# Int8 values transposed in pairs: a per-batch linear layer, layer norm and a quantised feed-forward on one core

## The chip, the cores and the metric

The kernel runs on one core of one Trainium2 chip. The metric is the time of one launch in microseconds (us) of device time. Three runs of the kernel before took 373.23, 369.0 and 368.7 us; the median is 369.0 us.

## What is computed

There are 8 batches of 256 tokens with 1024 features. Each batch picks one of 16 weight matrices by its id; the result is normalised, then goes through two linear layers whose inputs and weights are rounded to 255 levels with one scale per row, with a gelu between them. The input is added at the end.

```
w = weight[adapter_ids]                      # (8, 1024, 1024), float32
y = einsum('bij,bkj->bik', x, w)             # x: (8, 256, 1024)

def fake_quant(x):                           # one scale for each row
    s = maximum(max(abs(x), -1) / 127.0, 1e-8)
    return clip(round(x / s), -127, 127) * s

h = layernorm(y) * gamma + beta
h = einsum('bti,oi->bto', fake_quant(h), fake_quant(w1)) + b1
h = gelu(h, approximate=False)
h = einsum('bti,oi->bto', fake_quant(h), fake_quant(w3)) + b3
return x + h
```

## The kernel before, in words

**Sizes.** Tokens are cut into `TT` = 2 tiles of 128 rows, features into `CB` = 8 blocks of 128 columns, outputs into `KH` = 2 halves of 512, which is one PSUM bank of float32.

**First layer.** x and w are each split into a high part (the engine's float32r format) and the rest, and a product is three matmuls, hi\*hi, hi\*lo and lo\*hi (`products`, lines 1080 to 1082). A weight matrix is 4 units of 256 output rows; each unit has two pieces (`k` = 0, 1). For batches 2 to 7 a unit is loaded by SP (`load_unit`, line 285), transposed from `w_nat` into PSUM (`t_ps`) by VectorE in 32x32 blocks (`transpose_w`, line 803), copied to `w_hi` by ScalarE (`split_w`, line 574) and subtracted into `w_lo` by VectorE (`low_w`, line 809). x goes the same way (lines 296, 818, 580), except that GpSimd subtracts (`low_x`, line 483). For batches 0 and 1 TensorE transposes in float32 (`transpose_first`, lines 1173 and 1186).

**Norm.** ScalarE copies a half of y out of PSUM (`copy_y`, line 589), VectorE takes the statistics, GpSimd works out the scale and shift (`normalisers`), ScalarE applies them (`normalise`, line 593), and GpSimd multiplies by gamma and adds beta (`scale_and_shift`, lines 458 and 460).

**Quantisation.** VectorE takes the maximum of each row and its inverse (`scales_h`, `scales_g`, `max_prep` and `scales_prep`). The rounding is one instruction that multiplies by the inverse and adds MAGIC = 12582912.0, after which the low 16 bits of each float32 are the rounded value as an int16. It is ScalarE's for h and g (`round_h` line 601, `round_h_last` line 607, `round_g` line 622, and lines 707 and 711 in the last period) and GpSimd's for the 16 tiles of 128 rows of w1 and w3 (`round_prep`, line 489). TensorE transposes those low halves as bf16 bit patterns, 8 blocks of 128x128 for each tile of 128 rows (`transpose_tile`, line 1111), into one PSUM bank of 1024 16-bit words. ScalarE copies the bank as int16 to bf16 (`take_h` line 613 for two tiles at once, `take_g` line 627, `take_prep` line 639, `take` line 685 in the last period) into `q_t` or `w_q`. The products of the two linear layers are bf16 matmuls (`product_half`, line 1134): `ffn1` of h with w1, `ffn2` of g with w3.

**After the products.** `rescale1` (VectorE, line 876) scales the first product, `add_b1` (GpSimd, line 478) adds the bias, `gelu` (ScalarE, line 618) follows; `scale_ffn2` (ScalarE, line 632) scales the second, and `finish` (GpSimd, lines 466 and 469) multiplies by the row of weight scales and adds x + b3, which `residual` made (line 474). `store` (SP, line 359) writes it out.

**Order.** Each engine has its own list, written out by hand, and engines wait for each other by semaphores only. Batches 0 and 1 and the preparation of w1 and w3 stand in a start part written out step by step. Then comes a loop `period(p)` for p = 2 to 6, in which the first layer of batch p and p+1 and the feed-forward of batch p-1 are interleaved, and then a last period in which batches 6 and 7 are finished. In a period GpSimd runs `low_x(p+1, 0)`, `add_b1(p-1, 0)`, `residual`, `normalisers`, `low_x(p+1, 1)`, `add_b1(p-1, 1)`, two `scale_and_shift`, two `finish`. On SP the load of unit 1 of batch p+2 stands behind the store of the first tile of batch p-1. On TensorE a period is 8 pieces of the first layer, four transposed tiles (two of h, two of g) and the four products of the feed-forward:

```
            def period(p):                      # TensorE
                piece(p, 2, 0)
                transpose_h(p - 1, 0)
                transpose_h(p - 1, 1)
                piece(p, 2, 1)
                ffn1(p - 1, 0)
                ...
                piece(p + 1, 0, 0)
                transpose_g(p - 1, 0)
                piece(p + 1, 0, 1)
                ffn2(p - 1, 0)
```

Of the kernel before, what the change touches and what calls it, by code (L numbers as in the profile page):

```python
# [5 lines left out]
F32 = mybir.dt.float32  # L6
F32R = mybir.dt.float32r
BF16 = mybir.dt.bfloat16
I16 = mybir.dt.int16
# [5 lines left out]
P = 128  # L15
# [6 lines left out]

MAGIC = 12582912.0


def adaln_ffn_kernel(nc, x, ids, weight, gamma, beta, w1, b1, w3, b3, out):
# [27 lines left out]
    RT = D // P  # L54
    PREP = 2 * RT
# [6 lines left out]
    CONSTS = 7  # L62
# [3 lines left out]
    with ExitStack() as ctx:  # L66
# [30 lines left out]
        magic = sb("magic", [P, 1], F32)  # L97
# [34 lines left out]

        a_ps = psum("a_ps", [P, TT, BANK])
# [141 lines left out]
        def _(sp):  # L275
# [109 lines left out]
            load_prep((2, 4))  # L385
# [5 lines left out]
            load_prep((3, 5))  # L391
            load_rows_of_w((1,))
            load_prep((6,))
            load_rows_of_w((2, 5))
# [3 lines left out]
            load_prep((7, 8, 9))  # L398
            load_rows_of_w((4, 6, 7))
            load_prep((12, 10))  # L400
# [3 lines left out]
            load_prep((15, 14))  # L404
# [32 lines left out]
        def _(pool):  # L437
# [48 lines left out]
            def round_prep(tiles):  # L486
                for i in tiles:
                    pool.wait_ge(wq_inv_ready, part_of(i) + 1)
                    pool.tensor_scalar(prep_slot[i], prep_slot[i], wq_inv[:, i:i + 1], magic[:],
                                       ALU.mult, ALU.add).then_inc(wq_rounded, 1)  # L490

            def period(p):
# [6 lines left out]
                for t in range(TT):  # L499
                    scale_and_shift(p, t)  # L500
                for t in range(TT):
                    finish(p - 1, t)
# [3 lines left out]
            pool.memset(magic[:], MAGIC).then_inc(consts_ready, 1)  # L506
# [12 lines left out]
            round_prep((0, 1, 2, 3, 4, 5, 6))  # L519
# [5 lines left out]
            round_prep((9, 10, 11, 12))  # L525
# [5 lines left out]
            round_prep((14, 15))  # L531
# [28 lines left out]
        def _(act):  # L560
# [35 lines left out]
            def round_h(f, t):  # L596
                act.wait_ge(h_inv_ready, TT * f + t + 1)
                if isinstance(f, int) and f == 0:
                    act.wait_ge(first_transposed, first_piece(10, 0) + 1)
                wait_past(act, h_transposed, TT * (f - 1) + t + 1)  # L600
                act.activation(h_r[:, t, :], rows_of(f)[:, t, :], ACT.Identity, scale=h_inv[:, t:t + 1], bias=magic[:]
                               ).then_inc(h_rounded, 1)

            def round_h_last(t):
                act.wait_ge(h_inv_ready, TT * LAST + t + 1)
                act.wait_ge(h_transposed, TT * (LAST - 1) + t + 1)
                act.activation(h_r[:, t, :], y[:, t, :], ACT.Identity, scale=h_inv[:, TT + t:TT + t + 1], bias=magic[:]
                               ).then_inc(h_rounded, 1)
# [38 lines left out]
            def period(p):  # L647
                both(p + 1, 0)
                take_h(p - 1)
                split_x(p + 1, 0)  # L650
                both(p + 1, 1)
# [24 lines left out]
            def last_period():  # L676
# [6 lines left out]
                def take(ready, n, bank, blocks, done):  # L683
                    act.wait_ge(ready, n)
                    act.activation(blocks, transposed(bank, I16), ACT.Copy).then_inc(done, 1)
# [15 lines left out]
                for half in range(KH):  # L701
# [5 lines left out]
                act.activation(a_last[:, 0], a_last[:, 0], ACT.Identity, scale=g_inv[:, TT:TT + 1], bias=magic[:]  # L707
                               ).then_inc(g_rounded, 1)
                take(g_transposed, TT * LAST + 1, t_ps[:, 1, 0], q_last[:, 1, 0], g_t_ready)
                act.wait_ge(g_inv_ready, TT * LAST + 2)  # L710
                act.activation(a_last[:, 1], a_last[:, 1], ACT.Identity, scale=g_inv[:, TT + 1:TT + 2], bias=magic[:]
                               ).then_inc(g_rounded, 1)
# [659 lines left out]
```

## Time and profile before

| | |
|---|---|
| runs, us | 373.23, 369.0, 368.7 (median 369.0) |
| span of the profiled execution, us | 372.5 |
| TensorE (PE) busy | 341.4 us, 92% of the span, 1854 records |
| weight loads (PEld) busy | 235.9 us, 63% |
| VectorE (DVE) busy | 285.5 us, 77% |
| GpSimd (POOL) busy | 263.4 us, 71% |
| ScalarE (ACT) busy | 227.1 us, 61% |
| chain of waits | POOL 41%, issue 22%, DMA 13%, DVE 11%, PE 7%, SP's queue 3%, ACT 2% |

The profiled execution has no time of its own beside its span; the span is 0.7 us below the first of the three runs and 3.5 us above the median. "Issue" in the chain of waits is time in which an engine waited for nothing that the profile shows.

In the views below times are counted from the start of the span. A line of the timeline gives start and length in us, engine, line of the kernel, operation, what is written and read, the count of merged instructions and, in brackets, how long the engine sat idle before it and what ended the wait. The length of merged matmuls includes the end of the last one, which overlaps the next instruction; the pace is the distance from start to start. A few matmul records are missing, so that 16 matmuls can show as 15.

### The profile page before, as it was taken

The page shows a single profiled execution, that of the slowest core. Times are in us where ns is not written, and L with a number is a line of the kernel's source. Part 1 is how long each engine was busy: PE and PEld are TensorE (multiplying, and loading weights), DVE is VectorE, ACT ScalarE, POOL GpSimd, SP SyncE. Part 2 cuts the span into 40 slices and gives each one's busy share as a digit, 9 for nine tenths or more (in the row PEclk, how much of TensorE's full clock was granted, in tenths as well). Part 3 has the DMA queues.
Part 4 walks back from the last instruction along what each step waited for, and adds up shares of the span by engine and source line. Part 5 has one row for each costly group of instructions (what it writes and reads, how often), then busy time and mean ns, then how long its engine had stood idle before and what let it go on. Part 6 is the DMA issues. An engine that isn't in the chain of part 4 may idle for free.

```text
span 372.5 us, 5769 instructions
## 1 busy us (share of the span) xinstructions
PE 341.4 (92%) x1854; PEld 235.9 (63%) x1880; DVE 285.5 (77%) x344; ACT 227.1 (61%) x232; POOL 263.4 (71%) x164
## 2 busy tenths in 40 slices
PE   6898899996976999999999999999899989999885
PEld 6787788754763666666665666566566666674442
DVE  1459698886946777798778886888779687999866
ACT  2433476854888647773777658755777477625651
POOL 1402259841998579995999599968997699946831
PEclk9999999999899999999999999999999999999989
DMA  6999998695950899539971999099925990150014
GB/s 186 352 347 352 410 280 164 147 246 117 241 99 0 199 276 218 100 119 294 221 154 63 299 223 203 0 268 244 220 56 158 288 229 0 58 171 1 0 55 172
DMA packets 46203, 67.35 MB, mean 181 GB/s; under 512 B 2918, under 2 KB 37734, under 8 KB 46186
## 3 DMA queue, kind: packets, MB, share of 16 engines
q1 hardware_dynamic: 46186, 67.14, 68.8%
q8 instruction: 9, 0.15, 0.2%
q14 instruction: 8, 0.07, 0.1%
HBM read 58.74 MB, written 8.39 MB: 180 GB/s over the span
## 4 chain that ended last, share of the span: by engine, by line
POOL 41%; issue 22%; DMA 13%; DVE 11%; PE 7%; SPq 3%; ACT 2%; POOLq 0%; DVEq 0%
POOL y L458 8%; POOL x_res L474 7%; POOL o L466 6%; POOL y L460 5%; DMA x_res<-in_L_ffn_w 5%; POOL a L478 4%; POOL x_lo L483 4%; POOL o L469 3%; DMA w_scale_row<-in_L_ffn_w 3%; PE t_ps L1134 2%; DMA h_r<-in_L_cond_weight 2%; DVE x_nat L917 2%; DMA x_t<-in_L_ffn_b 2%; DVE wq_max L861 2%; DMA w_nat<-in_L_cond_weight 2%
## 5 line engine op out<-in xcount | busy, mean ns | idle before, releaser
L1080 PE MATMUL a_ps<-w_hi,x_hi 128*128 128x512 f32 x256 | 107.5, 420 | 2.4 <-DVE w_lo L794 1.2
L1082 PE MATMUL a_ps<-w_hi,x_lo 128*128 128x512 f32 x256 | 100.8, 394 | 0.0
L1081 PE MATMUL a_ps<-w_lo,x_hi 128*128 128x512 f32 x256 | 100.7, 393 | 0.0
L1134 PE MATMUL f_ps<-w_q,q_t 128*128 128x512 bf16 x377 | 88.1, 379 | 9.7 <-ACT q_t L627 8.2
L1134 PEld LDWEIGHTS f_ps<-w_q,q_t 128*128 128x128 bf16 x400 | 37.1, 98 | 57.5 <-ACT q_t L627 12.5
L803 DVE STREAM_TRANSPOSE t_ps<-w_nat 128x1024 f32<-128x1024 f32 x48 | 57.5, 1238 | 11.7 <-DMA w_nat<-in_L_cond_weight 11.5
L809 DVE TENSOR_TENSOR w_lo<-t_ps,w_hi 128x1024 fp32r<-128x1024 f32 x48 | 57.2, 1219 | 8.9 <-ACT w_hi L574 8.7
L574 ACT ACTIVATE w_hi<-t_ps 128x1024 fp32r<-128x1024 f32 x48 | 49.0, 1023 | 21.9 <-DVE t_ps L803 21.1
L1080 PEld LDWEIGHTS a_ps<-w_hi,x_hi 128*128 128x128 f32 x256 | 48.5, 189 | 15.7 <-ACT y L589 3.2
L1082 PEld LDWEIGHTS a_ps<-w_hi,x_lo 128*128 128x128 f32 x256 | 48.5, 189 | 10.7
L1081 PEld LDWEIGHTS a_ps<-w_lo,x_hi 128*128 128x128 f32 x256 | 48.6, 190 | 9.0
L478 POOL TENSOR_TENSOR a<-a,rows 128x1024 f32<-128x1024 f32 x14 | 33.4, 2385 | 19.7 <-DVE a L876 17.5
L483 POOL TENSOR_TENSOR x_lo<-x_t,x_hi 128x1024 fp32r<-128x1024 f32 x12 | 28.7, 2395 | 20.8 <-ACT x_hi L580 20.8
L474 POOL TENSOR_TENSOR x_res<-x_res,rows 128x1024 f32<-128x1024 f32 x14 | 33.4, 2412 | 0.0
L466 POOL TENSOR_TENSOR o<-o,w_scale_row 128x1024 f32<-128x1024 f32 x12 | 28.5, 2379 | 3.7 <-ACT o L632 3.7
L469 POOL TENSOR_TENSOR o<-o,x_res 128x1024 f32<-128x1024 f32 x12 | 29.6, 2465 | 0.9
L460 POOL TENSOR_TENSOR y<-y,rows 128x1024 f32<-128x1024 f32 x12 | 28.7, 2391 | 0.9
L458 POOL TENSOR_TENSOR y<-y,rows 128x1024 f32<-128x1024 f32 x12 | 28.6, 2382 | 0.0
L852 DVE TENSOR_REDUCE g_max<-a 128x1 f32<-128x1024 f32 x14 | 17.0, 1218 | 14.8 <-ACT a L618 14.8
L844 DVE TENSOR_REDUCE h_max<-y 128x1 f32<-128x1024 f32 x14 | 17.1, 1218 | 14.6 <-POOL y L460 14.6
L618 ACT ACTIVATE a<-a 128x1024 f32<-128x1024 f32 x14 | 14.8, 1056 | 16.4 <-POOL a L478 16.4
L569 ACT ACTIVATE w_hi<-t_ps 128x1024 fp32r<-128x1024 f32 x14 | 14.2, 1027 | 17.1 <-PE t_ps L1173 11.0
(151 smaller groups left out, 503.1 us busy)
## 6 DMA issues: line engine op xcount, KB each, us to landing
w_nat<-in_L_cond_weight SPq DMA_DIRECT2D x96, 256.0 KB, 6.5
x_res<-in_x SPq DMA_DIRECT2D x7, 1024.0 KB, 6.3
out<-o SPq DMA_DIRECT2D x14, 512.0 KB, 3.1
x_nat<-in_x SPq DMA_DIRECT2D x24, 256.0 KB, 9.9
w_nat<-in_L_cond_weight SPq DMA_DIRECT2D x10, 512.0 KB, 8.9
w_q<-in_L_ffn_w SPq DMA_DIRECT2D x4, 512.0 KB, 7.9
h_r<-in_L_cond_weight SPq DMA_DIRECT2D x4, 512.0 KB, 6.7
w_scale_row<-in_L_ffn_w SPq DMA_DIRECT2D x3, 512.0 KB, 10.3
```

The source lines that it names most:

```text
L458: pool.tensor_tensor(row, row, gamma_row, ALU.mult).then_inc(gamma_done, 1)
L460: pool.tensor_tensor(row, row, beta_row, ALU.add).then_inc(h_ready, 1)
L466: pool.tensor_tensor(o[:, t, :], o[:, t, :], w_scale_row[:, 1, :], ALU.mult).then_inc(out_scaled, 1)
L474: pool.tensor_tensor(x_res[:, t, :], x_res[:, t, :], b3_row, ALU.add).then_inc(x_b3_ready, 1)
L478: pool.tensor_tensor(a[:, t, :], a[:, t, :], b1_row, ALU.add).then_inc(ffn1_biased, 1)
L574: act.activation(part_of_unit(w_hi, u, k), piece_bank(k), ACT.Copy).then_inc(w_hi_ready, 1)
L803: dve.transpose(piece_bank(k).rearrange("p c (kb s) -> p kb c s", s=BLK), w_nat[:, u % 2].rearrange("p kb (c r) -> p kb c r", r=BLK)[:, :, ...
L809: dve.tensor_tensor(part_of_unit(w_lo, u, k), piece_bank(k), part_of_unit(w_hi, u, k).bitcast(F32), ALU.subtract).then_inc(w_lo_ready, 1)
L1080: pe.matmul(ps, hi, w_hi[:, u, c], start=begin, stop=False)
L1081: pe.matmul(ps, hi, w_lo[:, u, c], start=False, stop=False)
L1082: last = pe.matmul(ps, lo, w_hi[:, u, c], start=False, stop=end)
L1134: last = pe.matmul(ps[:, half, :], q[:, c, :], w[:, c, half_of(half)], start=c == 0, stop=c == CB - 1)
```

## The change

Rounded values are written as int8 by the rounding instruction itself: it multiplies by the inverse scale and the write converts, with no constant added. Two neighbouring bytes make one 16-bit word, so that a tile of 128 rows is 512 words, and TensorE transposes 4 blocks of 128x128 words in place of 8. ScalarE copies the transposed words out byte by byte: block 2c + b takes byte b of each word of block c, so it reads every second byte of PSUM and writes bf16. Activations and weights get the same order of rows in the product. `take_h` finds both tiles in one bank. h and g lie in byte ranges of `h_r`, so that `a` is no longer overwritten by the rounding. The constant `magic` and its memset go. Calls on several tiles are written out one by one; the order of the steps on each engine stays.

```diff
-I16 = mybir.dt.int16
+I8 = mybir.dt.int8
...
+    PACK = 2
-    CONSTS = 7
+    CONSTS = 6
...
+        bytes_of = [h_r[:, t, :].bitcast(I8) for t in range(TT)]
+        h_8 = [row[:, 0:D] for row in bytes_of]
+        g_8 = [row[:, D:2 * D] for row in bytes_of]
+        g_8_last = [row[:, 2 * D:3 * D] for row in bytes_of]
+        prep_8 = [slot.bitcast(I8)[:, 0:D] for slot in prep_slot]
...
-        def transposed(bank, dtype):
-            return bank.bitcast(dtype).rearrange("p (c k) -> p c k", k=P)
+        WORDS = D // PACK // PACK
+        def words_of(bank, t=0):
+            return bank[:, WORDS * t:WORDS * (t + 1)].bitcast(BF16).rearrange("p (c k) -> p c k", k=P)
+        def bytes_in(bank, tiles=1):
+            return bank[:, 0:WORDS * tiles].bitcast(I8).rearrange("p (c k b) -> p c b k", k=P, b=PACK)
+        def blocks_in(q):
+            return q.rearrange("p (c b) k -> p c b k", b=PACK)
...
-                    pool.tensor_scalar(prep_slot[i], prep_slot[i], wq_inv[:, i:i + 1], magic[:],
-                                       ALU.mult, ALU.add).then_inc(wq_rounded, 1)
+                    pool.tensor_scalar(prep_8[i], prep_slot[i], wq_inv[:, i:i + 1], None, ALU.mult).then_inc(wq_rounded, 1)
...
-            pool.memset(magic[:], MAGIC).then_inc(consts_ready, 1)
...
-                act.activation(h_r[:, t, :], rows_of(f)[:, t, :], ACT.Identity, scale=h_inv[:, t:t + 1], bias=magic[:]
-                               ).then_inc(h_rounded, 1)
+                act.activation(h_8[t], rows_of(f)[:, t, :], ACT.Identity, scale=h_inv[:, t:t + 1]).then_inc(h_rounded, 1)
...
-                act.activation(q_t[:].rearrange("p t c k -> p (t c k)"),
-                               f_ps[:].bitcast(I16).rearrange("p h n -> p (h n)"), ACT.Copy).then_inc(h_t_ready, 1)
+                act.activation(blocks_in(q_t[:].rearrange("p t c k -> p (t c) k")), bytes_in(f_ps[:, 0], TT), ACT.Copy
+                               ).then_inc(h_t_ready, 1)
...
-                act.activation(a[:, t, :], a[:, t, :], ACT.Identity, scale=g_inv[:, t:t + 1], bias=magic[:]
-                               ).then_inc(g_rounded, 1)
+                act.activation(g_8[t], a[:, t, :], ACT.Identity, scale=g_inv[:, t:t + 1]).then_inc(g_rounded, 1)
...
-                act.activation(q_t[:, t], transposed(f_ps[:, 0], I16), ACT.Copy).then_inc(g_t_ready, 1)
+                act.activation(blocks_in(q_t[:, t]), bytes_in(f_ps[:, 0]), ACT.Copy).then_inc(g_t_ready, 1)
...
-                    act.activation(w_q[i // RT][:, :, rows_of_tile], transposed(f_ps[:, i % 2], I16), ACT.Copy
+                    act.activation(blocks_in(w_q[i // RT][:, :, rows_of_tile]), bytes_in(f_ps[:, i % 2]), ACT.Copy
...
-            def transpose_tile(src, bank, done):
-                halves = src.bitcast(BF16).rearrange("p (k two) -> p k two", two=2)[:, :, 0]
-                blocks = transposed(bank, BF16)
-                for c in range(CB):
-                    last = pe.transpose(blocks[:, c, :], halves[:, c * P:(c + 1) * P], ident_16[:])
+            def transpose_tile(src, blocks, done):
+                words = src.bitcast(BF16)
+                for c in range(CB // PACK):
+                    last = pe.transpose(blocks[:, c, :], words[:, c * P:(c + 1) * P], ident_16[:])
                 last.then_inc(done, 1)
...
-                transpose_tile(h_r[:, t, :], f_ps[:, t], h_transposed)
+                transpose_tile(h_8[t], words_of(f_ps[:, 0], t), h_transposed)
...
-                transpose_tile(a[:, t, :], f_ps[:, 0], g_transposed)
+                transpose_tile(g_8[t], words_of(f_ps[:, 0]), g_transposed)
```

The last period's rounding, transposing and copying change in the same way, with `g_8_last` for the last batch's g.

## Rows read from the trace of the kernel before

**Rows 1.** The page, busy time, share of the span and instructions of each engine.
```profile
PE 341.4 (92%) x1854; PEld 235.9 (63%) x1880; DVE 285.5 (77%) x344; ACT 227.1 (61%) x232; POOL 263.4 (71%) x164
```

**Rows 2.** Stretches: from:to, length, PE busy (records), granted clock, DMA share, GB/s.
```profile
92.90:96.30 3.40, 3.40 (x10) 0.50 0.67 184
211.14:250.80 39.66, 38.20 (x191) 1.00 0.78 183
355.70:359.10 3.40, 3.40 (x15) 0.50 0.00 0
```

**Rows 3.** Timeline of one loop period, GpSimd, SP's queue and VectorE.
```profile
214.32 2.42 POOL L478 TENSOR_TENSOR a<-a,rows 128x1024 f32<-128x1024 f32 x1 [1.29 <-DVE a L876]
239.40 2.39 POOL L469 TENSOR_TENSOR o<-o,x_res 128x1024 f32<-128x1024 f32 x1
...
242.96 1.85 SPq L285 DMA_DIRECT2D w_nat<-in_L_cond_weight  x4
250.78 2.39 DVE L803 STREAM_TRANSPOSE t_ps<-w_nat 128x1024 f32<-128x1024 f32 x2 [1.75 <-DMA w_nat<-in_L_cond_weight]
254.53 2.40 POOL L478 TENSOR_TENSOR a<-a,rows 128x1024 f32<-128x1024 f32 x1 [1.85 <-DVE a L876]
```

**Rows 4.** Waits of SP's queue: us in total, times, longest.
```profile
SPq L359 <- POOL o L469: 123.1, 12, 26.1
```

**Rows 5.** Timeline of the same period, TensorE and ScalarE.
```profile
233.21 0.62 PE L1111 MATMUL f_ps<-ident,a 128*128 128x128 bf16 x8
233.63 0.48 PE L1080 MATMUL a_ps<-w_hi,x_hi 128*128 128x512 f32 x1
...
240.94 0.50 PE L1080 MATMUL a_ps<-w_hi,x_hi 128*128 128x512 f32 x1 [0.30 <-ACT y L589]
245.45 1.87 ACT L613 ACTIVATE q_t<-f_ps 128x2048 bf16<-128x2048 int16 x1
247.75 3.40 PE L1134 MATMUL f_ps<-w_q,q_t 128*128 128x512 bf16 x15
```

**Rows 6.** Groups by line: busy us, mean ns of one, idle before and its releaser.
```profile
L601 ACT ACTIVATE h_r<-y,magic,h_inv 128x1024 f32<-128x1024 f32 x12 | 14.9, 1244 | 11.3 <-DVE h_inv L840 11.3
L632 ACT ACTIVATE o<-f_ps,g_scale 128x1024 f32<-128x1024 f32 x12 | 13.3, 1109 | 2.3 <-PE f_ps L1134 2.3
L639 ACT ACTIVATE w_q<-f_ps 128x1024 bf16<-128x1024 int16 x16 | 16.0, 1023 | 6.2 <-PE f_ps L1111 6.2
L489 POOL TENSOR_SCALAR w_q<-w_q,wq_inv,magic 128x1024 f32<-128x1024 f32 x4 | 4.8, 1202 | 16.1 <-DVE wq_inv L840 16.1
L460 POOL TENSOR_TENSOR y<-y,rows 128x1024 f32<-128x1024 f32 x12 | 28.7, 2391 | 0.9
L505 POOL MEMSET ident<- 128x128 bf16 x1 | 0.2, 205 | 0.0
L504 POOL MEMSET ident<- 128x128 f32 x1 | 0.2, 205 | 0.3 <-POOLq L1362 0.3
```

**Rows 7.** Timeline of the start part, four engines.
```profile
70.89 1.25 ACT L601 ACTIVATE h_r<-y_first,magic,h_inv 128x1024 f32<-128x1024 f32 x1
88.08 1.22 DVE L861 TENSOR_REDUCE wq_max<-w_scale_row 128x1 f32<-128x1024 f32 x1 [1.56 <-DMA w_scale_row<-in_L_ffn_w]
104.16 1.07 PE L1111 MATMUL f_ps<-ident,y_first 128*128 128x128 bf16 x16
116.92 2.35 POOL L466 TENSOR_TENSOR o<-o,w_scale_row 128x1024 f32<-128x1024 f32 x1 [0.92 <-ACT o L632]
```

**Rows 8.** ScalarE in the start part, the same columns as rows 2 with ACT busy.
```profile
97.09:116.84 19.75, 17.40 (x17) 1.00 0.52 112
```

**Rows 9.** Timeline of the last period.
```profile
355.37 3.29 PE L1134 MATMUL t_ps<-w_q,q_t 128*128 128x512 bf16 x8 [2.74 <-ACT q_t L685]
358.46 0.94 PE L1111 MATMUL t_ps<-ident,w_nat 128*128 128x128 bf16 x8
359.23 1.89 PE L1134 MATMUL t_ps<-w_q,q_t 128*128 128x512 bf16 x8
```

More of the change, by code:

```diff
@@ L397, in _ @@
             load_rows_of_w((3,))
-            load_prep((7, 8, 9))
-            load_rows_of_w((4, 6, 7))
-            load_prep((12, 10))
+            load_prep((7,))
+            load_prep((8,))
+            load_prep((9,))
+            load_rows_of_w((4,))
+            load_rows_of_w((6,))
+            load_rows_of_w((7,))
+            load_prep((12,))
+            load_prep((10,))
             load_unit(2, 1)
@@ L498, in period @@
                 add_b1(p - 1, 1)
[L499 to L502, printed above, removed]
+                scale_and_shift(p, 0)
+                scale_and_shift(p, 1)
+                finish(p - 1, 0)
+                finish(p - 1, 1)
             pool.memset(ident[:], 0.0).then_inc(consts_zeroed, 1)
             pool.memset(ident_16[:], 0.0).then_inc(consts_zeroed, 1)
-            pool.memset(magic[:], MAGIC).then_inc(consts_ready, 1)
             pool.memset(minus_half[:], -0.5).then_inc(consts_ready, 1)
@@ L518, in _ @@
                 pool.partition_broadcast(rows[:, k], rows_1[k]).then_inc(rows_ready, 1)
-            round_prep((0, 1, 2, 3, 4, 5, 6))
+            round_prep((0,))
+            round_prep((1,))
+            round_prep((2,))
+            round_prep((3,))
+            round_prep((4,))
+            round_prep((5,))
+            round_prep((6,))
             normalisers_of(0)
@@ L647, in period @@
             def period(p):
-                both(p + 1, 0)
+                split_w(p + 1, 0, 0)
+                split_w(p + 1, 0, 1)
                 take_h(p - 1)
                 split_x(p + 1, 0)
-                both(p + 1, 1)
+                split_w(p + 1, 1, 0)
+                split_w(p + 1, 1, 1)
                 gelu(p - 1, 0)
@@ L684, in take @@
                     act.wait_ge(ready, n)
-                    act.activation(blocks, transposed(bank, I16), ACT.Copy).then_inc(done, 1)
+                    act.activation(blocks_in(blocks), bytes_in(bank), ACT.Copy).then_inc(done, 1)
                 take_h(f)
@@ L756, in _ @@
             split_x(2, 0)
-            both(2, 1)
+            split_w(2, 1, 0)
+            split_w(2, 1, 1)
             gelu(0, 0)
@@ L884, in period @@
             def period(p):
-                both(transpose_w, p + 1, 0)
-                both(low_w, p + 1, 0)
+                transpose_w(p + 1, 0, 0)
+                transpose_w(p + 1, 0, 1)
+                low_w(p + 1, 0, 0)
+                low_w(p + 1, 0, 1)
                 transpose_x(p + 1)
-                both(transpose_w, p + 1, 1)
+                transpose_w(p + 1, 1, 0)
+                transpose_w(p + 1, 1, 1)
                 rescale1(p - 1, 0)
-                both(low_w, p + 1, 1)
+                low_w(p + 1, 1, 0)
+                low_w(p + 1, 1, 1)
                 scales_g(p - 1, 0, a[:, 0, :], 0)
@@ L894, in period @@
                 rescale1(p - 1, 1)
-                both(transpose_w, p + 1, 2)
+                transpose_w(p + 1, 2, 0)
+                transpose_w(p + 1, 2, 1)
                 low_w(p + 1, 2, 0)
@@ L899, in period @@
                 scales_h(p, 0, 0)
-                both(transpose_w, p + 1, 3)
+                transpose_w(p + 1, 3, 0)
+                transpose_w(p + 1, 3, 1)
                 scales_h(p, 1, 1)
-                both(low_w, p + 1, 3)
+                low_w(p + 1, 3, 0)
+                low_w(p + 1, 3, 1)
                 statistics(p + 1, 0)
@@ L1037, in _ @@
             scales_h(0, 1, 1)
-            both(transpose_w, 2, 0)
+            transpose_w(2, 0, 0)
+            transpose_w(2, 0, 1)
             low_w(2, 0, 0)
@@ L1061, in _ @@
             scales_h(1, 0, 0)
-            both(low_w, 2, 3)
+            low_w(2, 3, 0)
+            low_w(2, 3, 1)
             scales_h(1, 1, 1)
@@ L1250, in last_period @@
                 pe.wait_ge(y_copied, UNITS * LAST + TT + 1)
-                transpose_tile(h_r[:, 0, :], a_ps[:, 0], h_transposed)
+                transpose_tile(h_8[0], words_of(a_ps[:, 0]), h_transposed)
                 product_half(q_t[:, 1], w_q[0], t_ps[:, 0], 1, ffn1_done)
@@ L1315, in _ @@
             piece(1, 0, 0)
-            prepare((4, 5))
+            prepare((4,))
+            prepare((5,))
             piece(1, 0, 1)
```

69 lines of the change are left out of this document (40 added, 29 removed).

## Prediction

> **What bounds the kernel now.** I read the page's busy shares first: TensorE at 92% of the span against VectorE's 77% looks like the bound [rows 1], and the loop seems to agree, since a period of 39.66 us holds 38.20 us of TensorE work at full clock [rows 2]. If that were all, each transpose taken away would come off the time. So the second view is the timeline of one loop period, read for what each engine waits on. GpSimd starts `add_b1(0)` at 214.32 and then runs without a gap that matters to the end of the first `finish` at 239.40 + 2.39 = 241.79, some 27.5 us. SP issues the load of unit 1 of the next batch at 242.96, VectorE sits idle until that load has landed and starts its transposes at 250.78, and GpSimd's next `add_b1(0)`, which waits for VectorE's rescaled product, starts at 254.53 [rows 3]. That is a closed ring of 254.53 - 214.32 = 40.2 us: 27.5 GpSimd, 9.0 store, issue and DMA, 3.75 VectorE. The other four periods of the loop begin the same way. SP's waits confirm the joint: its queue stood 123.1 us behind the `finish` [rows 4], with the load of unit 1 queued right behind the store. TensorE is not in this ring. It runs nearly as long as the ring does, and falls into step once a period, where its next first-layer piece waits for a ScalarE copy that itself waits on GpSimd's rows (at 240.94) [rows 5]. So in the loop TensorE is nearly full, but it follows.
>
> The start part is loads first (VectorE waits on a landing at 88.08), then from about 92 to 117 TensorE, ScalarE and GpSimd side by side, at whose end GpSimd waits 0.92 us for ScalarE's `scale_ffn2` [rows 7]. The last period is one chain through all engines, ending in TensorE's last products.
>
> **The change, part by part.**
>
> *Transposes.* Eight of them take 233.63 - 233.21 = 0.42 us from their start to the next piece [rows 5], about 53 ns each; four cost half, so a tile saves 0.21 us. There are 16 weight tiles, 16 of h and 16 of g: 48 tiles, 10.1 us of TensorE time in all. The new source is contiguous where the old one took every second 16-bit word; both give 128 columns of 16 bits, and I keep the price per transpose. Where it counts:
> - Loop, five periods, four tiles each: 0.84 us a period. Nothing in the ring waits for it; TensorE waits longer for the copies instead. 0.
> - Start before 88: the tile transposes lie between waits for loads. What can pass on is that `round_h(0, 1)` at 70.89, which releases the loads of the last w3 tiles, comes after copies that wait for TensorE, with some three tiles ahead of it. Its own gain below included, 0 to 0.8 us; as the landing at 88.08 also depends on loads that do not move, I take 0.3.
> - Start, 92 to 117: seven weight tiles (9 to 15) are transposed, among them two in the 16 of 104.16, so TensorE gets 1.5 us ahead. GpSimd can gain at most its 0.92 us wait [rows 7], for it is busy back to back before that. Bounds 0 and 0.92; I take 0.8, since ScalarE's own list then comes last. As the first store leaves earlier by this, the loop begins earlier by it.
> - Last period: one tile at 358.46 stands between two products, at half clock, 359.23 - 358.46 = 0.77 us [rows 9]; half goes, 0.38. One more stands before the last batch's second tile's product, at full clock: 0.21. The others there end before a wait. 0.59 in all; bounds 0 and 0.8.
>
> *ScalarE's rounding.* It took 1244 ns with a scale and a bias tile; the same function with the scale alone takes 1109 ns [rows 6], so 0.135 us less. The output is int8, which no row shows. Bounds: 0.2 less to 0.9 more (the latter if bytes were written at half speed, by the 0.86 us that 1024 elements more add, 1.87 against 1.023 [rows 5, 6]). I take 0.135 less, nearest to the same function's row. On the path lie two, both in the last period (h of the last tile, g of batch 6): 0.27. In the loop h and g's rounding lies beside the ring.
>
> *ScalarE's copies out of PSUM.* The element count stays; the read goes from contiguous int16 (1023 ns for 1024) [rows 6] to every second byte. Bounds: same, or half rate at +0.86 us a copy. I take the same, because stepping two bytes touches no more memory than the int16 did. The other end is a rival.
>
> *GpSimd's rounding of weights.* 1202 ns with two operations and two scalar operands; its two-input operation of the same size takes 2391 ns [rows 6], so the time follows what is read, and a bf16 memset takes the 205 ns of a float32 one [rows 6]. Bounds: 1.1 and 2.4 us. I take 1.2, no change. Most of the 16 end well before what waits on them; those for tiles 13 to 15, between 94 and 101, are in GpSimd's back-to-back stretch.
>
> *The rest.* One memset of a single column less, g rounded into `h_r` rather than in place, calls written out singly and one more register load on SP: all behind waits for loads, or without a new wait. The new buffer adds no semaphore. 0; if the extra SP step counted, tenths of a us.
>
> *Clock.* The granted clock fell to one half for 3.4 us at 92.9 and at 355.7 [rows 2], each time after TensorE had sat idle, the second after a wait of 2.74 us [rows 9] behind ScalarE and VectorE. The change lengthens such waits slightly, it does not remove them. A fall costs half of 3.4, 1.7 us of TensorE time. I leave both in place; one that vanished, or one more, is a bound of 1.7 either way.
>
> Sum: 0.3 + 0.8 + 0.59 + 0.27 = 2.0 us. It is worked out against an execution with a span of 372.5, 3.5 above the median; the ring's 40.2 against a period's 39.66 [rows 2, 3] is the kind of difference that it is made of. I take the difference off the median: 369.0 - 2.0 = **367.0 us**.
>
> **The rivals.**
>
> *TensorE sets the pace after all.* For it: 38.20 of 39.66 us busy [rows 2]. Then all 48 tiles count: 369.0 - 10.1 = 358.9, faster by 2.7%. Against it: the load, the two VectorE steps and `finish` have no TensorE in them, and GpSimd, whose wait it would have to shorten, waits for VectorE, which waits for a DMA.
>
> *Byte reads out of PSUM at half rate, slower than before.* Place: ScalarE's copies. In the loop `take_h` would end at 247.32 + 1.7 = 249.0 against the product's start at 247.75 [rows 5], about 1.3 us late. The first product can stand that (it is done by 251.15 and VectorE comes to it at 250.78 + 2.39 = 253.17 [rows 3, 5]); for the second I have 0 to 1.3 and take 0.4 us a period, 2.0 in all. In the start part six weight copies and the first of g, 7 x 0.86 = 6.0 us, meet 19.75 - 17.40 = 2.35 us of idle [rows 8]; 3.6 reach GpSimd. In the last period the copy that ended the 2.74 us wait [rows 9] adds 0.86 and two later ones about 0.5. 7.0 us: 367.0 + 7.0 = 374.0. It decides from about 0.25 us a copy, where it eats the 2.0 gained. For it: no row reads with a step. Against it: the int16 copy runs at the pace of float32 copies in the trace. The Trainium skill speaks for this rival, Advanced Engine Details and Errata, section PSUM Cachelines: the lines are 8 bytes, and "every two consecutive elements should be contiguous for best throughput". By that rule the new copies are the slow kind; the step is inside one line, though, and no row here shows a stepped read, so the trace neither confirms nor denies it.
>
> *GpSimd converts to int8 slowly.* Each rounding at the 2.4 us of its dearer operation, 1.2 more. The three on the path give 3.6 us; of the first nine, three stand before the first norm and can hold the loads behind `round_h(0, 1)` by up to 3 more. 370.6 to 373.6, say 372. Against it: the memset rows, and that one operation of two is gone.
>
> **How the numbers follow.** The forecast, a small gain through start and end alone, has 0.74; TensorE's pace 0.10; byte reads 0.08; GpSimd's conversion 0.08. The forecast's own bounds, all gains at their ends and the clock's 1.7 one way, reach from 364 to 371. I stretch to 363.5 and 372.0, which takes in half of GpSimd's rival and leaves out TensorE's pace and the byte reads: some 0.2 in all. 2% is 7.4 us, about what a measurement of this kernel can tell from no change. Faster by that is TensorE's pace, 0.10. Slower by that needs either slow rival at over its stated price, 0.04. Within 2%: 0.86.
>
> **What would show it.** Right: loop periods still 39.6 to 40.2 us with the same GpSimd and DMA joints, TensorE's records 192 fewer, its busy time some 10 us less and its idle time larger by about as much, the copies at 1.0 us, ScalarE's rounding near 1.1, GpSimd's at 1.2, and the loop entered about 1 us earlier. Wrong: loop periods shorter by 0.8 (TensorE's pace), copies of 1.9 us, or GpSimd rounding at over 1.5 us. A third fall of the clock, as TensorE idles more, would also show the sum short.

## The result, and the profile after

The change made the kernel slower: a median of 381.54 us (four runs, 380.74 to 383.4) against 371.12 us for the kernel before in runs alternated with it, a ratio of 1.031 with a 95% interval of 1.027 to 1.035 (one disturbed run of the kernel before, 472.58 us, is in its median but not in the ratio; below too, medians are of all runs and ratios of undisturbed ones). The prediction had 367.0 us and a range up to 372.0, so it missed by 14.5 us, 9.5 of them outside the range, and the sign was wrong: "slower by over 2%" had a chance of 0.04. The profiled execution took 380.74 us with a span of 378.9.

The page after, busy time and instructions of each engine, then the granted clock in 40 slices:

```profile
PE 333.1 (88%) x1667; PEld 225.7 (60%) x1688; DVE 284.4 (75%) x344; ACT 224.4 (59%) x232; POOL 289.2 (76%) x163
...
PEclk9999999699998999999999999999999999999989
```

Against [rows 1], TensorE has 187 records and 8.3 us less, as the change intends, and ScalarE 2.7 us less. GpSimd, with one instruction fewer, is busy 25.8 us longer. That one number says where to look. The groups by line say which instruction it is (busy us, mean ns of one, then the idle time before them):

```profile
L513 POOL TENSOR_SCALAR w_q<-w_q,wq_inv 128x1024 int8<-128x1024 f32 x4 | 11.3, 2850 | 15.5 <-DVE wq_inv L873 15.5
...
L668 ACT ACTIVATE w_q<-f_ps 128x1024 bf16<-128x1024 int8 x16 | 16.0, 1020 | 6.0 <-PE f_ps L1152 6.0
L633 ACT ACTIVATE h_r<-y,h_inv 128x1024 int8<-128x1024 f32 x12 | 13.8, 1150 | 14.7 <-DVE h_inv L873 14.7
L643 ACT ACTIVATE q_t<-f_ps 128x2048 bf16<-128x2048 int8 x7 | 13.1, 1873 | 2.4 <-PE f_ps L1152 2.4
```

A weight tile's rounding on GpSimd went from 1202 ns [rows 6] to 2850 (the other buffers' groups, 2836 to 2852 ns, are alike): 1.65 us more, sixteen times, 26.4 us. Everything else the change touched is as priced or close: ScalarE's byte reads take 1020 and 1873 ns, as the int16 reads did [rows 5, 6]; its rounding takes 1150 ns.

The extra time lies before the loop alone: the loop's first `add_b1(0)` starts at 141.87 us, against 135.05 before, 6.8 us later, and the spans are 6.4 apart (the profiled execution of the kernel before was one of its slower ones). A stretch of the kernel after, one period (from:to, length, TensorE busy and records, granted clock, DMA share, GB/s):

```profile
178.20:217.70 39.50, 37.16 (x175) 1.00 0.79 183
```

The period is what it was, with a microsecond less of TensorE work in it [rows 2]; from one `add_b1(0)` to the next the loop takes 39.5 to 40.3 us, where it took 39.6 to 40.2. And its joints are the same. The timeline of one period, GpSimd, SP's queue and VectorE:

```profile
221.50 2.40 POOL L502 TENSOR_TENSOR a<-a,rows 128x1024 f32<-128x1024 f32 x1 [1.76 <-DVE a L909]
246.60 2.38 POOL L493 TENSOR_TENSOR o<-o,x_res 128x1024 f32<-128x1024 f32 x1
...
250.15 1.86 SPq L300 DMA_DIRECT2D w_nat<-in_L_cond_weight  x4
...
257.58 2.39 DVE L836 STREAM_TRANSPOSE t_ps<-w_nat 128x1024 f32<-128x1024 f32 x2 [1.35 <-DMA w_nat<-in_L_cond_weight]
261.32 2.40 POOL L502 TENSOR_TENSOR a<-a,rows 128x1024 f32<-128x1024 f32 x1 [1.44 <-DVE a L909]
```

From `add_b1(0)` to the end of `finish` 27.5 us, then 8.6 of store, issue and DMA, then 3.74 of VectorE: 39.8 us, against 27.5, 9.0 and 3.75 in [rows 3].

### The profile page after: what moved, and what is told of

Read it like the earlier page. It is cut to its first block, busy times and chain, and to the rows that moved or that the text cites. A ratio compares the mean times of both kernels' runs of the same rounds, so it can differ in the third digit from the quotient of the medians.

```text
span 378.9 us, 5398 instructions
## 1 busy us (share of the span) xinstructions
PE 333.1 (88%) x1667; PEld 225.7 (60%) x1688; DVE 284.4 (75%) x344; ACT 224.4 (59%) x232; POOL 289.2 (76%) x163
## 4 chain that ended last, share of the span: by engine, by line
POOL 49%; issue 20%; DMA 9%; DVE 9%; PE 6%; SPq 3%; ACT 2%; POOLq 0%; DVEq 0%; ACTq 0%
POOL y L482 7%; POOL x_res L498 7%; POOL o L490 6%; POOL y L484 5%; POOL a L502 5%; POOL x_lo L507 4%; POOL o L493 3%; DMA a<-in_L_ffn_w 3%; DMA w_scale_row<-in_L_ffn_w 3%; POOL w_scale_row L513 2%; PE t_ps L1175 2%; DMA h_r<-in_L_cond_weight 2%; DVE x_nat L957 2%; DMA x_t<-in_L_ffn_b 2%; POOL y L513 1%
## 5 line engine op out<-in xcount | busy, mean ns | idle before, releaser
L836 DVE STREAM_TRANSPOSE t_ps<-w_nat 128x1024 f32<-128x1024 f32 x48 | 57.5, 1238 | 10.1 <-DMA w_nat<-in_L_cond_weight 9.9
L606 ACT ACTIVATE w_hi<-t_ps 128x1024 fp32r<-128x1024 f32 x48 | 48.9, 1022 | 20.1 <-DVE t_ps L836 19.0
L648 ACT ACTIVATE a<-a 128x1024 f32<-128x1024 f32 x14 | 14.8, 1054 | 17.8 <-POOL a L502 17.8
L513 POOL TENSOR_SCALAR w_q<-w_q,wq_inv 128x1024 int8<-128x1024 f32 x4 | 11.3, 2850 | 15.5 <-DVE wq_inv L873 15.5
```

Source lines behind the costliest of these rows:

```text
L606: act.activation(part_of_unit(w_hi, u, k), piece_bank(k), ACT.Copy).then_inc(w_hi_ready, 1)
L836: dve.transpose(piece_bank(k).rearrange("p c (kb s) -> p kb c s", s=BLK), w_nat[:, u % 2].rearrange("p kb (c r) -> p kb c r", r=BLK)[:, :, ...
```

## The experiments

Three theories stood after this. A: GpSimd is slow because it writes int8. B: a term other than GpSimd is in it (h and g's bytes, or TensorE's idling). C: GpSimd is slow because its second operation is gone. (The expectation for m_forms, written before C had its name, calls it Theory B, together with a second suspicion, that input and output overlap.) In those for e1, e2 and e3 Theory A stands for GpSimd's rounding as the whole loss, whatever its reason. Ratios are to the kernel before, run beside each (369.98, 370.31, 369.85 and 370.3 us in the four sets).

**m_forms: single instructions.** A list of forms, run through three times, each instruction after the one before has ended; VectorE and ScalarE start only when GpSimd is done.

```diff
+then(pool.tensor_scalar(o_f32[:], src[:], scale[:], bias[:], ALU.mult, ALU.add))
+then(pool.tensor_scalar(o_f32[:], src[:], scale[:], None, ALU.mult))
+then(pool.tensor_scalar(o_bf16[:], src[:], scale[:], None, ALU.mult))
...
+then(pool.tensor_scalar(o_i8[:], src[:], scale[:], None, ALU.mult))
+then(pool.tensor_copy(o2_i8[:], src[:]))
...
+act.activation(a_f32[:], src[:], ACT.Identity, scale=scale[:])
+act.activation(a_i8[:], src[:], ACT.Identity, scale=scale[:])
```

> This kernel computes nothing of the reference: it loads one tile of 128x1024 float32, runs single instructions on it by form, and stores the tile unchanged. The changed kernel's trace has GpSimd's scaling with int8 output at 2.85 us where the float32 form took 1.20. Theory A, the type written sets the price: here the float32 forms take 1.2 us with one or with two scalar operands, the int8 form 2.85, also into a tile of its own, and the rewrite in place is no dearer. Theory B, it is the dropped second operation or the overlap of input and output: then the float32 form with one operation is slow as well, or the int8 form is fast where the output is a tile of its own. Open under A: whether bf16, int16 and int32 outputs cost as float32 or as int8; whether VectorE's and ScalarE's int8 outputs cost more than their float32 ones (ScalarE near 1.15 us, as in the changed kernel).

The groups by line of that kernel:

```profile
L75 POOL TENSOR_SCALAR o_i<-src,scale 128x1024 int8<-128x1024 f32 x3 | 8.5, 2845 | 0.3
L71 POOL TENSOR_SCALAR o_f<-src,scale 128x1024 f32<-128x1024 f32 x3 | 8.5, 2845 | 0.3
L72 POOL TENSOR_SCALAR o_bf<-src,scale 128x1024 bf16<-128x1024 f32 x3 | 8.5, 2844 | 0.3
...
L70 POOL TENSOR_SCALAR o_f<-src,scale,bias 128x1024 f32<-128x1024 f32 x3 | 3.6, 1193 | 4.9 <-DMA inplace<-in_L_ffn_w 4.7
L102 ACT ACTIVATE a_i<-src,scale 128x1024 int8<-128x1024 f32 x3 | 3.5, 1151 | 0.1
L100 ACT ACTIVATE a_f<-src,scale 128x1024 f32<-128x1024 f32 x3 | 3.5, 1150 | 0.1
...
L76 POOL CAST o_i<-src 128x1024 int8<-128x1024 f32 x3 | 3.1, 1037 | 0.2
```

Theory A falls: the multiply alone takes 2845 ns with float32, bf16 and int8 output alike, and the plain cast to int8 takes 1037 (int16 and int32 output take 2843 and 2844). So does the suspicion of overlap: the multiply to int8 in place takes 2845 as well. What is fast is the form with a multiply and an add. On ScalarE int8 output costs the same as float32.

**m_forms2: what makes the form fast.** The same with other operands.

```diff
...
+then(pool.tensor_scalar(o_i8[:], src[:], scale[:], zero[:], ALU.mult, ALU.add))
+then(pool.tensor_scalar(o_i8[:], src[:], scale[:], 0.0, ALU.mult, ALU.add))
+then(pool.tensor_scalar(o_i8[:], src[:], 1500.0, 0.0, ALU.mult, ALU.add))
+then(pool.tensor_scalar(o_i8[:], src[:], 1500.0, None, ALU.mult))
...
+then(pool.tensor_scalar(o_f32[:], src[:], scale[:], None, ALU.add))
```

> Single instructions again, nothing of the reference. The first such kernel showed GpSimd's scaling at 2.84 to 2.85 us for every output type where the second operation is left out, and 1.19 with it. Theory C, the missing second operation sets the price: the int8 output with a multiply and an add of a zero column takes 1.2 us, in place too. Rival, int8 with two operations is slow as well. Open: whether a constant in place of the zero column, or of the scale, keeps the 1.2 us, and whether an add alone is as slow as a multiply alone.

```profile
L78 POOL TENSOR_SCALAR o_f<-src,scale 128x1024 f32<-128x1024 f32 x3 | 8.5, 2842 | 0.3
L76 POOL TENSOR_SCALAR o_i<-src 128x1024 int8<-128x1024 f32 x3 | 8.3, 2772 | 0.3
...
L73 POOL TENSOR_SCALAR o_i<-src,scale,zero 128x1024 int8<-128x1024 f32 x3 | 3.6, 1190 | 0.3
...
L74 POOL TENSOR_SCALAR o_i<-src,scale 128x1024 int8<-128x1024 f32 x3 | 3.3, 1113 | 0.3
...
L75 POOL TENSOR_SCALAR o_i<-src 128x1024 int8<-128x1024 f32 x3 | 3.1, 1044 | 0.3
```

Over both kernels, every tensor-scalar form with two operations takes 1.04 to 1.20 us (1195 ns in place), every form with one 2.77 to 2.85, whatever type is written, whether the operand is a column or a constant, and whether the operation is a multiply or an add. Why one operation takes longer than two no run shows.

**e7_two_ops: the changed kernel with a neutral second operation.**

```diff
-pool.tensor_scalar(prep_8[i], prep_slot[i], wq_inv[:, i:i + 1], None, ALU.mult)
+pool.tensor_scalar(prep_8[i], prep_slot[i], wq_inv[:, i:i + 1], zero[:], ALU.mult, ALU.add)
...
+pool.memset(zero[:], 0.0).then_inc(consts_ready, 1)
```

> The changed kernel, with one thing more: GpSimd's rounding to int8 multiplies and then adds a column of zeros, so that it has two operations again. Theory C: each rounding falls from 2.85 to 1.2 us and the whole loss of 3.1% goes: ratio 0.993 to 1.003, the weights' shorter transposes being worth under 1 us. Rival, the byte layout itself costs (int8 output, stepped reads, idle TensorE): it stays above 1.02.

367.36 us, ratio 0.992 [0.989, 0.995]. An add of zero, with all the rest of the change left in, takes the whole loss away and leaves a gain, 3.0 us by medians, somewhat more than expected. It was run once more:

> The changed kernel with two operations in GpSimd's rounding once more, beside its sister with longer weight transposes on the same chip. Its first ratio was 0.9919 and that of the kernel with every transpose doubled 1.0018, 2.6 us apart by their medians, where the prediction's terms give 0.8 (start) + 0.6 (last period) = 1.4 and 0.3 more through the loads. Expected again 0.989 to 0.995, with loop periods of 39.6 to 40.5 us.

366.72 us, 0.991 [0.987, 0.994]. The group of roundings in this kernel:

```profile
L514 POOL TENSOR_SCALAR w_q<-w_q,wq_inv,zero 128x1024 int8<-128x1024 f32 x4 | 4.7, 1199 | 16.0 <-DVE wq_inv L876 16.0
```

**e10_one_op: the kernel before with one operation.** The reverse: nothing of the change but the missing operation. It leaves out the added constant, so that the low halves which are transposed are not the rounded weights.

```diff
-pool.tensor_scalar(prep_slot[i], prep_slot[i], wq_inv[:, i:i + 1], magic[:],
-                   ALU.mult, ALU.add).then_inc(wq_rounded, 1)
+pool.tensor_scalar(prep_slot[i], prep_slot[i], wq_inv[:, i:i + 1], None, ALU.mult).then_inc(wq_rounded, 1)
```

> The kernel before, whose weight rounding on GpSimd leaves out the add of the constant (the low halves that are transposed then are not the rounded weights, so this part of the computation is wrong). No byte anywhere. Theory C: the dropped operation alone makes 11 to 13 us, ratio 1.028 to 1.036. Rival: under 1.01, and the bytes are to blame.

384.5 us, 1.038 [1.032, 1.045], 14.2 us more than before, where 11 to 13 were expected; the group of roundings, float32 written as before:

```profile
L489 POOL TENSOR_SCALAR w_q<-w_q,wq_inv 128x1024 f32<-128x1024 f32 x4 | 11.4, 2854 | 16.6 <-DVE wq_inv L839 16.6
```

One operation of one instruction carries the loss, with no byte in the kernel.

**e1_hg_bytes and e2_w_bytes: each half of the change alone.** e1 keeps bytes for h and g and gives the weights their old rounding and eight transposes; e2 does the opposite.

```diff
 e1, against the changed kernel:
-pool.tensor_scalar(prep_8[i], prep_slot[i], wq_inv[:, i:i + 1], None, ALU.mult)
+pool.tensor_scalar(prep_slot[i], prep_slot[i], wq_inv[:, i:i + 1], magic[:], ALU.mult, ALU.add)
...
-transpose_tile(prep_8[i], words_of(f_ps[:, i % 2]), wq_transposed)
+transpose_halves(prep_slot[i], f_ps[:, i % 2], wq_transposed)
 e2, against the changed kernel:
-transpose_tile(h_8[t], words_of(f_ps[:, 0], t), h_transposed)
+transpose_tile(h_r[:, t, :], f_ps[:, t], h_transposed)
...
-transpose_tile(g_8[t], words_of(f_ps[:, 0]), g_transposed)
+transpose_tile(a[:, t, :], f_ps[:, 0], g_transposed)
```

> h and g as bytes, as in the changed kernel; the weights rounded by GpSimd in float32 with the constant added and transposed as eight blocks of 16-bit halves, as before, in the byte pairs' order of rows. Theory A (GpSimd's int8 rounding is the whole loss): the weights' share of the change is gone, so the time is that of the kernel before or a little under: 0 to 1 us less, ratio 0.997 to 1.00. Theory B (the loss lies in the loop or the last period, in the clock or in the copies out of PSUM): it stays slow, 375 us or more. The loop's periods stay at 39.6 to 40.2 us under both, if the ring of GpSimd, store, load and VectorE sets them.

> Only the weights as bytes, rounded by GpSimd straight to int8 and transposed as four blocks; h and g as before (their halves read in the byte pairs' order). Theory A: the whole loss is here, 9 to 12 us over the kernel before, ratio 1.025 to 1.032, and the loop is entered 6 to 8 us late. Theory B: no more than 3 us over it.

e1: 371.95 us, 1.004 [0.999, 1.009], no difference that it could show, though 0 to 1 us less was expected. e2: 382.26 us, 1.031 [1.025, 1.037], the whole loss. B falls for h and g: the 32 tiles whose transposes were halved there bring nothing measurable, as the loop ring says. What their bytes could cost is at most the upper end of e1's interval, 3.3 us; e9 below, all bytes with the TensorE work of before, narrows that to 0.5% (1.8 us).

**e3_pad: the time without the bytes.** The kernel before, with two extra operations ahead of each rounding, sized so that the three take about as long as one slow one.

```diff
+for width in (D, 384):
+    part = prep_slot[i][:, 0:width]
+    pool.tensor_scalar(part, part, 1.0, 0.0, ALU.mult, ALU.add).then_inc(padded, 1)
+    pads.append(1)
+    pool.wait_ge(padded, len(pads))
```

> The kernel before with nothing changed but that GpSimd, ahead of each of the 16 roundings, multiplies the tile by one and adds zero over 1024 and over 384 columns: 1.20 + 0.45 us more for each, the length that the int8 output added. Theory A, the loss is GpSimd's time alone: 9 to 12 us slower, as the changed kernel, plus the 1 us or so that the changed kernel got back by shorter transposes and roundings. Rival, the int8 form also disturbs others (VectorE, the DMAs) beyond its own length: this kernel stays under 6 us slower.

384.29 us, 1.035 [1.028, 1.041], again somewhat more than the 10 to 13 us expected. The pads took 2 x 0.782 = 1.56 us a rounding:

```profile
L494 POOL TENSOR_SCALAR w_q<-w_q 128x1024 f32<-128x1024 f32 (+1 forms) x8 | 6.3, 782 | 17.4 <-DVE wq_inv L848 17.1
```

So 25 us more of GpSimd work at these places cost 14.3 us at the end, and e10's 26.4 cost 14.2. The loss needs nothing but GpSimd's time; the rival of a disturbance beyond it falls.

**e5_swap: is the store in the ring?** In the kernel before, SP's load of the next batch's unit 1 goes ahead of the store that waits for `finish`.

```diff
-store(p - 1, 0)
 load_unit(p + 2, 1)
+store(p - 1, 0)
...
-store(0, 0)
 load_unit(3, 1)
+store(0, 0)
```

> The kernel before, with the load of unit 1 of the next batch but one ahead of the store of the first tile on SP's queue, in the loop and at its start. If the loop's period is the ring of GpSimd, store, load and VectorE, VectorE's wait for that load of 1.1 to 1.8 us a period goes, and the five periods shorten by 1 to 1.5 us each, 5 to 7 us in all, until TensorE's 38.2 us is the bound: ratio 0.980 to 0.987. If TensorE sets the period already, nothing moves.

362.87 us, 0.977 [0.969, 0.984], 7.4 us less, a little beyond the 5 to 7 expected. Its timeline, three engines:

```profile
207.21 2.40 POOL L478 TENSOR_TENSOR a<-a,rows 128x1024 f32<-128x1024 f32 x1
...
209.07 21.98 SPq L285 DMA_DIRECT2D w_nat<-in_L_cond_weight  x12
234.75 5.61 SPq L359 DMA_DIRECT2D out<-o  x2
...
241.91 2.34 DVE L803 STREAM_TRANSPOSE t_ps<-w_nat 128x1024 f32<-128x1024 f32 x2
245.61 2.40 POOL L478 TENSOR_TENSOR a<-a,rows 128x1024 f32<-128x1024 f32 x1
```

The loads now stand before the stores, VectorE starts its transposes at 241.91 without a wait, and the period is 245.61 - 207.21 = 38.4 us. The ring of the prediction was real: opened at that joint, the four intervals from one `add_b1(0)` of the loop to the next take 38.4 us each in place of 39.6 to 40.2, together 5.9 us less.

**e8_two_ops_swap: both together.** e7 with e5's order.

> The changed kernel with two operations in GpSimd's rounding and, on SP's queue, the load of unit 1 ahead of the first store. The swap alone gave 0.9765 and loop periods of 38.4 us, the second operation 0.9919. If the two gains lie in different places (loop; start and last period) they add: ratio 0.965 to 0.973, 358 to 360 us, the periods staying at 38.4 us, which GpSimd and VectorE now set. If the shorter transposes are worth something in the loop once its ring is shorter, the periods fall under 38.2 us and the ratio under 0.965.

358.98 us, 0.972 [0.965, 0.978], 2.8% faster than the kernel before and the fastest that was run. One period (columns as for the stretches above):

```profile
203.00:241.40 38.40, 37.11 (x174) 1.00 0.80 184
```

It is 38.4 us again, as in e5, with 1 us less of TensorE work than before the change, so the shorter transposes are worth nothing in the loop even then. What sets the period now was not tried.

**e9_two_ops_t_twice and e12_w_t_twice: what the transposes are worth.** e9 is e7 with every group of four transposes issued twice, e12 with those of the weight tiles alone.

```diff
 e9, against e7:
-for c in range(CB // PACK):
+for c in [*range(CB // PACK)] * 2:
 e12, against e7:
-for c in range(CB // PACK):
+for c in [*range(CB // PACK)] * times:
...
-transpose_tile(prep_8[i], words_of(f_ps[:, i % 2]), wq_transposed)
+transpose_tile(prep_8[i], words_of(f_ps[:, i % 2]), wq_transposed, 2)
```

> The changed kernel with two operations in GpSimd's rounding, and each group of four transposes issued twice, into the same place: TensorE has the work of the kernel before again, with all else as bytes. If the shorter transposes are worth 1.7 us, in the start part and the last period alone, this takes 1 to 2 us more than with them single, ratio 0.994 to 0.999 to the kernel before, and the loop's periods stay at 39.6 to 40.2 us. If TensorE's time passes on fully it takes 10 us more, ratio 1.02.

> As its sister, but each group of four transposes of a weight tile (the 16 in the start part) is issued twice; those of h and g stay single. If the shorter transposes gain in the start part, most of the difference is here: 1 to 2.5 us over its sister. If they gain in the loop or the last period, under 0.5 us.

e9: 369.79 us, 1.002 [0.999, 1.005]; e12: 370.85 us, 1.003 [0.999, 1.007]. Doubling the weight tiles' alone takes back all that e11 (0.991 [0.987, 0.994], run beside e12) had gained, 370.85 - 366.72 = 4.1 us by medians, where 1 to 2.5 were expected. e9 against e7 is 2.4 us by medians, but those two ran in different sets; by their ratios it is 0.010, 3.7 us. Doubling those of h and g as well adds nothing that shows. The gain of the change therefore comes from the weights' transposes in the start part; the terms of the last period are too small to be told from none.

## Why the prediction was wrong

**GpSimd's rounding: the step that failed.** It read "I take 1.2, no change", with bounds of 1.1 and 2.4. The measured value, 2.85, lies outside both. The reasoning failed in two places. "So the time follows what is read" was drawn from a two-operation instruction and a two-input one; neither says what an instruction with one operation takes, and there was no such row of that size. And "that one operation of two is gone" stood as evidence against the slow rival, while it was the cause. The rival named the right engine and line, for a reason that m_forms refuted: the conversion to int8 is free. I had bounded the new part of the instruction (the type) and taken the removed part as at worst neutral. The term stood in the sum at 0; it measured 14.8 us at the end (the changed kernel's median less e11's).

**What it costs: the path was short too.** The rival counted three roundings on the path, 3.6 us, and up to 3 us from the first nine, through the loads behind `round_h(0, 1)`. The changed kernel and e11, which differ in this instruction (and a column of zeros) alone, can be laid side by side. GpSimd in the changed kernel, start part:

```profile
34.27 11.34 POOL L513 TENSOR_SCALAR w_q<-w_q,wq_inv 128x1024 int8<-128x1024 f32 x4 [15.53 <-DVE wq_inv L873]
48.66 5.67 POOL L513 TENSOR_SCALAR y<-y,wq_inv 128x1024 int8<-128x1024 f32 x2 [3.05 <-DVE wq_inv L873]
...
71.35 2.38 POOL L484 TENSOR_TENSOR y_first<-y_first,rows 128x1024 f32<-128x1024 f32 x1
73.72 5.66 POOL L513 TENSOR_SCALAR x_res<-x_res,wq_inv 128x1024 int8<-128x1024 f32 x2
79.36 5.66 POOL L513 TENSOR_SCALAR o<-o,wq_inv 128x1024 int8<-128x1024 f32 x2
...
94.98 2.40 POOL L502 TENSOR_TENSOR a<-a,rows 128x1024 f32<-128x1024 f32 x1 [5.29 <-DVE a L909]
...
124.08 2.35 POOL L490 TENSOR_TENSOR o<-o,w_scale_row 128x1024 f32<-128x1024 f32 x1
```

And in e11:

```profile
34.74 4.75 POOL L514 TENSOR_SCALAR w_q<-w_q,wq_inv,zero 128x1024 int8<-128x1024 f32 x4 [15.97 <-DVE wq_inv L876]
49.79 2.38 POOL L514 TENSOR_SCALAR y<-y,wq_inv,zero 128x1024 int8<-128x1024 f32 x2 [10.30 <-DVE wq_inv L876]
...
64.66 2.40 POOL L485 TENSOR_TENSOR y_first<-y_first,rows 128x1024 f32<-128x1024 f32 x1
...
69.41 2.38 POOL L514 TENSOR_SCALAR o<-o,wq_inv,zero 128x1024 int8<-128x1024 f32 x2
...
86.23 2.38 POOL L503 TENSOR_TENSOR a<-a,rows 128x1024 f32<-128x1024 f32 x1 [3.44 <-DVE a L912]
...
111.31 2.35 POOL L491 TENSOR_TENSOR o<-o,w_scale_row 128x1024 f32<-128x1024 f32 x1 [0.92 <-ACT o L664]
```

The first four roundings (tiles 0 to 3) cost nothing: their 6.6 us shorten the wait that follows, 10.30 to 3.05. The next five (tiles 4 to 8) stand ahead of the end of GpSimd's norm of the second tile, and GpSimd has next to no wait there: the norm ends at 73.73 against 67.06, 6.7 us later. What hangs on it is the loads. ScalarE's `round_h(0, 1)`, SP's queue and VectorE in the changed kernel, then in e11:

```profile
76.39 1.15 ACT L633 ACTIVATE h_r<-y_first,h_inv 128x1024 int8<-128x1024 f32 x1
77.56 0.83 SPq L369 DMA_DIRECT2D y_first<-in_L_ffn_w  x2
81.07 0.45 SPq L369 DMA_DIRECT2D w_scale_row<-in_L_ffn_w  x1
91.24 1.22 DVE L894 TENSOR_REDUCE wq_max<-w_scale_row 128x1 f32<-128x1024 f32 x1 [1.15 <-DMA w_scale_row<-in_L_ffn_w]
```

```profile
69.92 1.15 ACT L636 ACTIVATE h_r<-y_first,h_inv 128x1024 int8<-128x1024 f32 x1 [0.26 <-DVE h_inv L876]
71.09 0.83 SPq L370 DMA_DIRECT2D y_first<-in_L_ffn_w  x2
75.15 0.45 SPq L370 DMA_DIRECT2D w_scale_row<-in_L_ffn_w  x1
82.53 1.18 DVE L897 TENSOR_REDUCE wq_max<-w_scale_row 128x1 f32<-128x1024 f32 x1
```

`round_h(0, 1)` reads the buffer that the loads overwrite, so they leave 6.5 us later, and the last of them 5.9. It then takes 10.1 us to land, and VectorE waits for it, where in e11 it had landed in at most 7.4; why it took longer is open. VectorE comes to it 8.71 us later, and `add_b1(0, 1)`, which needs what VectorE makes just after, 94.98 - 86.23 = 8.75 us later. The four roundings between (tiles 9 to 12, from 73.72 to 85.02) run beside this: GpSimd still waits 5.29 us for VectorE after them. The profile's chain of waits takes this way, through `round_h(0, 1)` and the landing and past tiles 9 to 12, in all four kernels with the longer work at the roundings (the changed one, e2, e3 and e10; landings of 10.1 to 12.5 us). From `add_b1(0, 1)` on GpSimd has no wait left: the last three roundings add 3 x 1.65 less the 0.92 of wait, 4.0, and the first scaling of a result comes 124.08 - 111.31 = 12.8 us later. The ends are 12.4 apart, 378.9 against 366.5.

So the last three I had as the path, rightly. The hold on the loads, where I allowed 3 us for the three roundings ahead of the first norm (tiles 4 to 6), carried 8.75, two thirds of the delay: the loads wait for the second tile's norm, behind tiles 7 and 8 as well, and the slower landing made it longer. An engine that idles for over a quarter of the span [rows 1] had no idle time to give in the 25 us (48.66 to 73.73) in which the price counted.

**The loop and its rival: right.** Periods of 39.5 to 40.3 us, with 37.2 of TensorE work in them. "TensorE sets the pace after all" (358.9) falls: 1 us less of TensorE a period moved no period, e1 shows nothing from 32 tiles, and e5 gains by moving a store.

**Price of a transpose: right, its worth in the start too small.** The timeline of the changed kernel has four from whose start to the next product it is 0.24 us:

```profile
356.84 0.40 PE L1152 MATMUL t_ps<-ident,h_r 128*128 128x128 bf16 x4
357.08 1.89 PE L1175 MATMUL a_ps<-w_q,q_t 128*128 128x512 bf16 x8
```

Priced at 0.21 us [rows 5]; in the start part it is 98.52 - 98.31 = 0.21. But I allowed 0.3 and 0.8 us for the start, 1.1 in all, where e12 and e9 give 2.4 to 4.1 us for the 16 weight tiles, 3.4 us of TensorE time by the price. Why nearly all of it, or more, reaches the end is not settled. In the traces of e11 and e12, whose spans are 3.3 us apart, `add_b1(0, 1)` stands at 86.23 and 88.08, and the first scaling at 111.31 and 113.33. So 1.9 us of the 3.3 are there by 86, before the stretch that I weighed heaviest, next to nothing is added in that stretch, and the rest appears in the loop, where e12 doubles nothing. One trace each can't tell TensorE's time from how the loads happened to land. GpSimd's wait before that scaling is the same 0.92 in e11 as before [rows 7], so the 0.8 us that I took from it wasn't collected there.

**ScalarE: right.** The rounding takes 1150 ns, 0.09 less than before where I said 0.135. The copies from every second byte take 1020 and 1873 ns against 1023 and 1.87 [rows 5, 6]; the rival at 374.0 has no cost to stand on; that its time came nearest to the measured one is chance. The Trainium skill, Advanced Engine Details and Errata, section PSUM Cachelines, on which it leaned, is not borne out for ScalarE's reads of a byte in two; the measurement decides.

**Last period and clock: about right.** From the last `add_b1` to the end it is 26.8 us before, 26.3 after and in e11: 0.5 us less, where 0.86 were forecast. The wait before the last products grew from 2.74 [rows 9] to 3.22:

```profile
362.18 1.27 PE L1175 MATMUL t_ps<-w_q,q_t 128*128 128x512 bf16 x4 [3.22 <-ACT q_t L716]
```

The granted clock still falls to half there (0.51 over the 3.4 us from 362.8), as before [rows 2]. In the start part of the changed kernel it was 0.50 from 65.9 for 6.8 us and from 117.1 for 3.4, where before it was so for 3.4 us from 92.9 [rows 2]: three falls in all, of which the prediction had named a third as a sign of a short sum. The longer fall began 0.5 us into a wait of TensorE for a rounding:

```profile
68.98 0.61 PE L1152 MATMUL f_ps<-ident,a 128*128 128x128 bf16 x4 [3.54 <-POOL a L513]
```

e11, with the fast rounding, has neither that wait nor a fall there (1.00 from 64 to 80 us), so I take this one for a consequence of the slow rounding; it was not tested apart. The loss doesn't need it: e10 lost as much with a granted clock of 1.00 in that stretch. Nor are such falls the slow rounding's alone: e5, with the fast one, had 0.50 to 0.52 from 113 to 119 us. The bound of one fall more or less, 1.7 us, was in the range.

**The sum without the failed step.** The prediction was 2.0 us for everything else. e7 and e11, which are the change without that step, gain 3.0 and 3.6 us by medians. There the sign was right and the size a little short, though not made up as forecast: nearly all of it is the weights' transposes in the start, priced at 1.1. The failed step alone, the changed kernel against e11, is 381.54 - 366.72 = 14.8 us.

## What to carry to other kernels

An instruction made simpler is a new instruction: price it by a row of exactly its form (number of operations, operands), and where no row has it, time it by itself before the kernel is built around it, or keep the old form with a neutral operand, here an add of zero. Count a price that changes on a shared engine in the stretch where that engine has no wait left, not by its share of the span, and follow what is released behind it, loads above all. And a store that waits for the end of a computation should not stand ahead of a load on one queue: moving it gave more (0.977) than the whole change with its fault mended (0.991).

## What the runs showed of the hardware

- On GpSimd a tensor-scalar instruction on 128x1024 float32 takes 2.77 to 2.85 us with one operation and 1.04 to 1.20 with two; on 128x512 it is 1.57 and 0.76. With constants in place of columns two operations take 0.15 less. The output type changes neither price (five types with one operation, float32 and int8 with two). A cast to int8 takes 1.04.
- ScalarE's activation with a column scale writes int8 in the 1.15 us of float32, and reads every second byte of PSUM in 1.02 us for 1024 elements, as it reads int16 side by side.
- On VectorE one multiply of 128x1024 float32 takes 0.75 us with float32, int16 and int8 output alike.
- TensorE does four 128x128 transposes of 16-bit words in 0.21 to 0.24 us at full clock, half of eight's 0.42 [rows 5], also when a word is two bytes that hold two numbers.
